# A two-part layer on one core: early rows from six routing groups, and their timetable one token tile to the front

## The chip, the core and the metric

The kernel runs on one core of a Trainium2 chip. A core has a matmul engine (TensorE, PE; its weight loads are listed as PEld), a vector engine (VectorE, DVE), an activation engine (ScalarE, ACT), GpSimd (POOL) and SyncE (SP), which here issues DMAs; 16 DMA engines move data between HBM and the on-chip memory SBUF. PE writes its results to eight PSUM banks. The metric is the device time of one execution in microseconds (us), lower is better.

## What is computed

Attention (a Nystroem form with landmarks, an iterated inverse and a convolution over the rows), then a mixture of eight experts, each with a residual. In the reference, cut to what matters:

```python
x = x + attention(layernorm(x))                   # x is 4 x 1024 x 256
h = layernorm(x)                                  # 4096 tokens of 256
logits = h @ router_w.T                           # 8 experts
routing_weights, selected = sparsemixer_eval(logits, 0.01)   # two experts for each token
for e in range(8):
    g = silu(h @ w_gate[e].T) * (h @ w_up[e].T)   # 512 wide
    out = out + dense_w[:, e:e + 1] * (g @ w_down[e].T)
x = x + out
```

All is in float32. Since each token goes to two of eight experts, 8192 rows are sorted by expert and computed in blocks.

## The kernel before

**Token loop.** The last third of the attention and the routing run together in `token_step(i)`, written out for each engine. Each batch of 1024 rows has 9 query tiles (CT = 9, QT = 36 in all). In step i PE computes the scores of query tile i (`c2_sim`, L1730), the convolution with the values of tile i - 2 (`c2_conv`, L1775), and the output product y of a row tile of 128 rows (`c2_y`, L1783, `y_step(m)` is the step of row tile m). Every ninth step (12, 21, 30) has no y tile. DVE takes the maxima and sums of the softmax (L1210, L1213, L1220, L1226), and adds y to the residual: that is x1(m), `rows_out`, L1111, with the statistics behind it. ACT takes the exponentials and moves the convolution out of PSUM, GpSimd weighs (`weigh`, L571) and adds the bias to the residual rows (`add_bias`, L577), which x1(m) waits for.

**Routing.** Row tiles form nine groups (`GROUPS`): 0 to 6 have four tiles, 7 and 8 have two. `DONE[g]`, called D in this document, is the step of the last y tile of group g: 7, 11, 16, 20, 25, 29, 34, 36, 38. `LATE` is 6. Behind it come, for groups 0 to 5: the deviations (`inverse_deviations`, DVE, L1124 to L1132) and the normalised rows (`norm_rows`, ACT, L774) in step D+1; on PE two pairs of transposes (`c2_tp`, L1743), h = 0 in D+2 and h = 1 in D+3, each with its logits (`c2_lg`, L1751); the choice of the experts (`choices`, DVE, L1165 to L1177, with the logits transposed back on PE, L1765) in step `CHOSEN` = D+4; the counts (`c2_counts`, PE, L1801) in `COUNTED` = D+5; the slots of the rows (`take_counts` and `slots`, DVE, L1153 and L1184 to L1203) in `PLACED` = D+6; and from there the scatter of the rows to their expert's region of xs_d in HBM (`scatter`, GpSimd, L585), two tiles in step `PLACED` and two in the next. `sent_at` moves those that fall in steps 35 to 37 one step on. Group 6 has its transposes in D+1 and D+2, and its choice, counts and slots in steps 36, 37 and 37.

**Early rows.** The expert with most rows after the first `EARLY + 1` groups (`choose_early`, DVE, L1233 to L1240, behind the slots of group `EARLY`) surely has `EROWS` rows by then: a whole number of 128-row tiles. Two steps behind `PLACED[EARLY]` SP loads this expert's weights and these rows (`first_rows`, L413 to L420), once the groups' scatters have landed. They are computed around the end of the token loop, while the last groups are still being placed.

**Experts.** The rest of the rows is computed in items, in an order fixed ahead (`KIND`), whose expert and address are read from tables: units (two 128-row tiles of one expert, two steps), tiles (128 rows, part-full, one step) and quads (four pieces of 32 rows, one step). `ITEMS` has the steps of each item, `NU` and `NT` the numbers of units and tiles that suffice for any routing. A step has gate and up products (`hidden`, L1887) and a down product (`down`, L1930), an item the transposes of its rows (`x_columns`, L1850). For a unit the gate and up products have 256 moving columns, for a tile 128 and twice as many instructions. DVE weighs the products (L1301), and GpSimd adds them to the output in HBM (`add_rows`, L606); an item's adds wait until those of the item ahead have landed.

With EARLY = 4, EROWS is 640: two units and one single tile (5 steps). Then come 22 units, 6 quads and 11 tiles, the last five items being tiles: 5 + 44 + 6 + 11 = 66 steps.

The order on each engine is the order of the code. What runs ahead is set by semaphores alone.

## Time and profile before

| | |
|---|---|
| median of three runs | 1118.95 us (1118.33 to 1119.6) |
| profiled execution | 1113.18 us, its span 1111.4 us |
| PE busy | 96% of the span |
| PEld, DVE, ACT, POOL busy | 77%, 58%, 29%, 27% |
| DMA | 68.27 MB, mean 61 GB/s |
| PE's chain: gate and up (L1887), down (L1930) | 221.9 us and 113.9 us |
| PE: scores L1730, y L1783, convolution L1775 | 129.7, 120.2 and 65.1 us |

The span runs from the first to the last instruction; times in the rows are us from its start. The token loop lies from about 410 to 724, the expert stage behind it. A row of a timeline merges neighbouring instructions of one kind. In brackets stands the idle time of the engine ahead of it and whose work ended it. PEclk is the granted share of TensorE's full clock.

### The profile page before, as it was taken

How to read it: one execution, taken by the hardware profiler on the slowest of the kernel's cores; microseconds unless marked ns; L12 is line 12 of the kernel's file. 1: busy time of each engine (PE TensorE's matmuls, PEld its weight loads, DVE VectorE, ACT ScalarE, POOL GpSimd, SP SyncE). 2: the span in 40 equal slices, each digit the busy share in tenths (PEclk: the TensorE clock that was granted, in tenths of full speed). 3: DMA queues.
4: the chain of work that ended last, by engine and by line, in shares of the span. 5: the costliest groups of instructions: out<-in, count | busy, mean ns of one | idle time of the engine just before them, and what ended most of it. 6: DMA issues, size and time to landing. Idle time of an engine off the chain costs nothing. (4 is left out here: it accounts for less than half of the span.)

```text
span 1111.4 us, 22942 instructions
## 1 busy us (share of the span) xinstructions
PE 1069.8 (96%) x9126; PEld 859.7 (77%) x9126; DVE 641.6 (58%) x1376; ACT 319.2 (29%) x471; POOL 301.2 (27%) x303
## 2 busy tenths in 40 slices
PE   4999999999999999999999999999999999999996
PEld 4888888888888756667766666788887877878895
DVE  7457756655558576677677777875334434343332
ACT  4433232222224423332332342331122122121210
POOL 6000000000020013225435435462332333333333
PEclk9999999999999999999999999999999999999999
DMA  9300000000300040321322224235423233333122
GB/s 336 127 1 1 1 1 1 1 1 1 97 3 0 2 191 20 106 67 64 126 80 68 97 66 129 87 134 103 86 48 49 46 45 52 49 51 46 20 30 24
DMA packets 48253, 68.27 MB, mean 61 GB/s; under 512 B 8225, under 2 KB 41505, under 8 KB 47137
## 3 DMA queue, kind: packets, MB, share of 16 engines
q1 hardware_dynamic: 34288, 46.83, 13.4%
q0 software_dynamic: 13440, 16.93, 9.2%
q10 hardware_dynamic: 432, 3.24, 0.7%
q8 instruction: 62, 1.02, 0.4%
q14 instruction: 31, 0.25, 0.1%
HBM read 41.43 MB, written 26.59 MB: 61 GB/s over the span
## 5 line engine op out<-in xcount | busy, mean ns | idle before, releaser
L1887 PE MATMUL ps<-mem 128*128 128x256 f32 (+1 forms) x1152 | 221.9, 345 | 0.0
L1887 PEld LDWEIGHTS ps<-mem 128*128 128x128 f32 x1152 | 190.1, 191 | 27.2 <-issue 7.5
L606 POOL DMA_INDIRECT out<-mem x60 | 102.6, 1710 | 188.8 <-DVE mem L1301 139.7
L571 POOL TENSOR_TENSOR mem<-mem,small 128x1024 f32<-128x1024 f32 x36 | 68.6, 1905 | 241.9 <-DVE small L1223 112.0
L1289 DVE TENSOR_TENSOR mem<-mem,ps 128x512 f32<-128x512 f32 x66 | 45.4, 687 | 150.5 <-PE ps L1887 129.8
L1730 PE MATMUL ps<-mem 128*128 128x512 f32 x288 | 129.7, 594 | 0.0
L1783 PE MATMUL ps<-mem 128*128 128x256 f32 x512 | 120.2, 388 | 0.0
L818 ACT ACTIVATE mem<-ps 128x512 f32<-128x512 f32 x66 | 39.4, 597 | 278.5 <-PE ps L1887 250.4
L1480 PE MATMUL ps<-mem 128*128 128x256 f32 x512 | 117.3, 382 | 0.6 <-ACT mem L692 0.6
L1930 PE MATMUL ps<-mem 128*128 x480 | 113.9, 380 | 1.8 <-DVE mem L1289 1.8
L1441 PE MATMUL ps<-mem 128*128 128x256 f32 x512 | 114.5, 380 | 0.0
L1783 PEld LDWEIGHTS ps<-mem 128*128 128x128 f32 x512 | 95.8, 192 | 16.3 <-issue 4.3
L1441 PEld LDWEIGHTS ps<-mem 128*128 128x128 f32 x512 | 95.6, 190 | 12.7 <-issue 0.3
L1480 PEld LDWEIGHTS ps<-mem 128*128 128x128 f32 x512 | 94.8, 190 | 13.5 <-issue 0.8
L1930 PEld LDWEIGHTS ps<-mem 128*128 128x128 f32 x480 | 88.3, 190 | 12.9 <-issue 2.5
L1730 PEld LDWEIGHTS ps<-mem 128*128 128x128 f32 x288 | 54.2, 190 | 54.8 <-issue 52.7
L585 POOL DMA_INDIRECT xs_d<-mem,idx x64 | 62.3, 974 | 40.2 <-DVE idx L1203 23.9
L1775 PEld LDWEIGHTS ps<-mem 128*64 128x64 f32 x1152 | 57.1, 137 | 18.3 <-issue 18.3
L1775 PE MATMUL ps<-mem 128*64 128x116 f32 x1152 | 65.1, 266 | 0.8 <-POOL mem L571 0.8
L1318 DVE COPY mem<-mem 128x2048 f32 x51 | 62.0, 1235 | 5.9 <-issue 3.1
L793 ACT ACTIVATE mem<-ps 128x928 f32<-128x928 f32 (+2 forms) x36 | 31.5, 874 | 103.0 <-PE ps L1775 103.0
L1301 DVE TENSOR_SCALAR mem<-ps,mem 128x256 f32<-128x256 f32 x66 | 29.7, 480 | 46.7 <-PE ps L1930 46.4
(237 smaller groups left out, 1388.0 us busy)
## 6 DMA issues: line engine op xcount, KB each, us to landing
mem<-w_gu SPq DMA_DIRECT2D x9, 1024.0 KB, 5.6
mem<-xs_d SPq DMA_DIRECT2D x22, 260.0 KB, 2.8
mem<-x SPq DMA_DIRECT2D x8, 512.0 KB, 8.2
mem<-x SPq DMA_DIRECT2D x32, 128.0 KB, 2.3
out<-mem SPq DMA_DIRECT2D x32, 128.0 KB, 1.7
mem<-w_down SPq DMA_DIRECT2D x8, 512.0 KB, 5.5
xnt_d<-mem ACTq DMA_DIRECT2D x3, 1056.0 KB, 5.3
mem<-xnt_d SPq DMA_DIRECT2D x3, 1056.0 KB, 4.9
```

The costliest lines, as they stand in the source:

```text
L571: pool.tensor_tensor(a1[:, u], ex[:, u].rearrange("p (h c) -> p h c", h=H), ri[:, 16 * u:16 * u + 16].unsqueeze(2).to_broadcast([P, H, M]) ...
L585: pool.indirect_dma_start(out=xs_d, out_offset=bass.IndirectOffsetOnAxis(ap=idx[:, u, v, c:c + 1].bitcast(U32), axis=0), in_=xd[:, u, v, c ...
L606: pool.indirect_dma_start(out=out_rows, out_offset=bass.IndirectOffsetOnAxis(ap=rows_to.bitcast(U32), axis=0), in_=ys[:, r % YRING], in_of ...
L1289: dve.tensor_tensor(hid[:, n % 2], sil[:, n % 2], bank(2 + n % 2), ALU.mult).then_inc(s("m_hid"), 1)
L1318: dve.tensor_copy(v, w_gu_s[:, e]).then_inc(s("m_w"), 1)
L1441: mm = pe.matmul(bank(t // 2)[:, t % 2 * 2 * P:(t % 2 + 1) * 2 * P], xnts[b][:, k, HALO + P * t:HALO + P * t + P], g3c[:, b, k, j * P:(j + ...
L1480: mm = pe.matmul(bank(6)[:, k * 2 * P:(k + 1) * 2 * P], xna[:, b, t, k * P:(k + 1) * P], e3s[m % 4][:, t], start=(t == 0), stop=(t == RT - 1))
L1730: mm = pe.matmul(bank(2 * u + half), xnt2[b % 2][:, k, TO * t:TO * t + P], g1c[:, b, k, 512 * half:512 * half + 512], start=(k == 0), stop ...
L1775: mm = pe.matmul(bank(4, 2)[c:c + 64, (h // 2) * P:(h // 2) * P + TO], a1[:, q % 2, h], band[:, h], start=True, stop=True)
L1783: mm = pe.matmul(bank(6)[:, 0:D], cvt[:, j, at_:at_ + P], pm[:, b, j], start=(j == 0), stop=(j == J - 1))
L1887: mm = pe.matmul(bank(2 * c + n % 2)[:, i * size:(i + 1) * size], w[:, k, c, f * P:(f + 1) * P], xst[:, a % 2, k, 0:size], start=(k == 0), ...
L1930: mm = pe.matmul(bank(down_bank(a, b))[:, 0:D], hid[:, u, i * size + b * P:i * size + (b + 1) * P], w_d_s[:, e, f], start=(f == 0), stop=( ...
```

## The change

`EARLY` becomes 5: six groups are placed before the early rows are taken, so `EROWS` is 768, six tiles in three units. The rows left shrink by 128, so `NT` goes from 11 to 10 (the last four items are tiles); NU and the quads stay. The steps are 6 + 44 + 6 + 10 = 66. `choose_early` moves to group 5's slots, the early loads to two steps behind them. `CHOSEN`, `COUNTED` and `PLACED` of groups 0 to 5 are each one step less, and their transposes and logits stand where those of group 6 stood: h = 0 in D+1, h = 1 in D+2.

```diff
-EARLY = 4
+EARLY = 5
...
-CHOSEN = [i + 4 for i in DONE[:LATE]] + [QT, QT + 2, QT + 4]
-COUNTED = [i + 5 for i in DONE[:LATE]] + [QT + 1, QT + 3, QT + 5]
-PLACED = [i + 6 for i in DONE[:LATE]] + [QT + 1, QT + 4, QT + 5]
+CHOSEN = [i + 3 for i in DONE[:LATE]] + [QT, QT + 2, QT + 4]
+COUNTED = [i + 4 for i in DONE[:LATE]] + [QT + 1, QT + 3, QT + 5]
+PLACED = [i + 5 for i in DONE[:LATE]] + [QT + 1, QT + 4, QT + 5]
...
-                return i + 1 if QT - 1 <= i <= QT + 1 else i
+                return i + 1 if QT <= i <= QT + 1 else i
...
@@ token_step of the tensor engine (ACT's norm_columns move alike)
-                for h in range(2):
-                    for g in groups_at(DONE[:LATE], i - 2 - h):
-                        c2_tp(g, h)
                 for g in groups_at(CHOSEN[:LATE], i):
                     c2_logit_rows(g)
-                if i == DONE[LATE] + 2:
-                    c2_tp(LATE, 1)
-                    pe.wait_ge(s("c2_sub"), QT - 1)
-                    c2_lg(LATE, 0)
+                for g in groups_at(DONE[:LATE + 1], i - 2):
+                    c2_tp(g, 1)
+                    if g < LATE:
+                        bank6_read(i)
+                    else:
+                        pe.wait_ge(s("c2_sub"), QT - 1)
+                    c2_lg(g, 0)
                 if 0 <= i - 2 < QT:
                     c2_conv(i - 2)
-                if i == DONE[LATE] + 1:
-                    c2_tp(LATE, 0)
-                if i == DONE[LATE] + 2:
-                    c2_lg(LATE, 1)
+                for g in groups_at(DONE[:LATE + 1], i - 1):
+                    c2_tp(g, 0)
+                for g in groups_at(DONE[:LATE + 1], i - 2):
+                    c2_lg(g, 1)
                 bank6_read(i)
-                for h in range(2):
-                    for g in groups_at(DONE[:LATE], i - 2 - h):
-                        c2_lg(g, h)
...
             hidden(0, 4)
             down(3)
+            hidden(1, 4)
+            hidden(0, 5)
             x_columns(3)
-            hidden(1, 4)
+            down(4)
+            hidden(1, 5)
```

ACT gets `gate_out(5)` and DVE `hidden_out(5)` for the sixth early step. The kernel after has other line numbers: DVE's 2 lower (L1111 is L1109), PE's 1 lower in the token loop.

Three places in the order of the engines. First DVE in step 35, before, from the subtraction of the maxima of step 34 to the slots of group 5:

```order
L1213 TENSOR_TENSOR mem<-ps,small 128x1024 [waits c2_a1,dve_chain]
L1111 TENSOR_TENSOR mem<-ps,mem 128x256 [waits x1_out3,c2_norm,c2_xrb,c2_y]
L1116 BN_STATS small<-mem 128x6 [waits c2_x1]
...
L1132 SCALAR_TENSOR_TENSOR small<-small 128x4 [waits dve_chain]
L1153 COPY mem<-ps 128x64 [waits d_cnt]
L1220 TENSOR_REDUCE small<-mem 128x16 [waits c2_exp]
L1226 RECIPROCAL small<-small 128x16 [waits dve_chain]
L1210 TENSOR_REDUCE small<-ps 128x16 [waits c2_sim]
L1213 TENSOR_TENSOR mem<-ps,small 128x1024 [waits c2_a1,dve_chain]
L1184 TENSOR_TENSOR mem<-mem 128x64 [waits d_exp]
```

And the same place after, from the subtraction of step 34 to x1(27) of step 35:

```order
L1211 TENSOR_TENSOR mem<-ps,small 128x1024 [waits c2_a1,dve_chain]
L1182 TENSOR_TENSOR mem<-mem 128x64 [waits d_exp]
...
L1201 CAST idx<-mem 128x2x4 [waits dve_chain]
L1231 TENSOR_TENSOR small<-run,small 128x8
...
L1238 SCALAR_TENSOR_TENSOR small<-small 128x8 [waits dve_chain]
L1109 TENSOR_TENSOR mem<-ps,mem 128x256 [waits x1_out3,c2_norm,c2_xrb,c2_y]
L1114 BN_STATS small<-mem 128x6 [waits c2_x1]
```

The slots of group 5 (17 instructions) and the choice of the early expert (8) stand ahead of x1(27) now; the slots stood behind the subtraction of step 35, the choice in step 31.

Second GpSimd in steps 34 to 38 (L571 weighs, L577 adds a bias, L585 scatters a tile to one of its two experts), as the difference:

```order
 L571 TENSOR_TENSOR mem<-mem,small 128x1024
 L577 TENSOR_TENSOR mem<-mem 128x256
+L585 DMA xs_d<-mem,idx 33920x260 x4
 L571 TENSOR_TENSOR mem<-mem,small 128x1024
 L577 TENSOR_TENSOR mem<-mem 128x256
 L585 DMA xs_d<-mem,idx 33920x260 x4
-L577 TENSOR_TENSOR mem<-mem 128x256
-L585 DMA xs_d<-mem,idx 33920x260 x4
-L577 TENSOR_TENSOR mem<-mem 128x256
+L571 TENSOR_TENSOR mem<-mem,small 128x1024
+L577 TENSOR_TENSOR mem<-mem 128x256 x3
 L585 DMA xs_d<-mem,idx 33920x260 x16
```

Group 5's scatters stand in steps 34 and 35, where they stood in 36 and 37; those of groups 6 to 8 stay.

Third SP, where the early weights (w_gu) and early rows (xs_d) are loaded, in the kernel after (L409 stores a row tile, L400 loads down weights):

```order
L400 DMA mem<-w_down 128x1024 x2
L409 DMA out<-mem 128x256
L414 TENSOR_LOAD early
L414 ISA x2
L415 ISA
L415 DMA mem<-w_gu 128x2x1024
L419 TENSOR_LOAD early
L419 ISA x2
L420 ISA
L420 DMA mem<-xs_d 128x6x260
L409 DMA out<-mem 128x256 x3
```

The two early loads stood ahead of the stores of row tiles 26 and 27, in step 33, with 5 tiles of rows; they stand now in step 36, behind the store of row tile 28.

## Rows read from the trace of the kernel before

**Rows 1.** The page: busy us of each engine, share of the span, instructions.

```profile
PE 1069.8 (96%) x9126; PEld 859.7 (77%) x9126; DVE 641.6 (58%) x1376; ACT 319.2 (29%) x471; POOL 301.2 (27%) x303
```

**Rows 2.** Timeline, PE, expert stage: start us, us, engine, line, operation, operands, count.

```profile
1042.31 3.62 PE L1887 MATMUL ps<-mem 128*128 128x256 f32 x16
...
1053.11 3.62 PE L1887 MATMUL ps<-mem 128*128 128x256 f32 x16
...
1074.77 3.73 PE L1887 MATMUL ps<-mem 128*128 128x128 f32 x32
...
1080.29 3.73 PE L1887 MATMUL ps<-mem 128*128 128x128 f32 x32
```

**Rows 3.** Timeline, PE, end of the token loop; in brackets idle time and releaser.

```profile
672.27 0.60 PE L1743 MATMUL ps<-ids,mem 128*128 128x128 f32 x4
...
702.15 0.66 PE L1743 MATMUL ps<-ids,mem 128*128 128x128 f32 x4
...
715.99 0.41 PE L1801 MATMUL ps<-mem,tri 128*128 128x32 f32 x2 [0.48 <-DVE mem L1111]
...
721.48 0.66 PE L1743 MATMUL ps<-ids,mem 128*128 128x128 f32 x4 [1.33 <-ACT mem L774]
722.92 1.03 PE L1759 MATMUL ps<-rw,mem 128*128 128x8 f32 x8 [0.78 <-ACT mem L782]
723.80 0.93 PE L1850 MATMUL ps<-ids,mem 128*128 128x128 f32 x4
```

**Rows 4.** Windows of core 0: length, busy us of PE, PEld, DVE, ACT, POOL, PEclk, DMA, GB/s.

```profile
112.00:114.00 2.00, 0.49 (x3) 0.20 (x2) 1.59 (x3) 0.97 (x2) 0.00 (x0) 1.00 0.00 0
720.00:724.00 4.00, 1.89 (x15) 1.53 (x15) 3.56 (x20) 2.03 (x3) 3.06 (x5) 1.00 0.28 100
724.00:728.00 4.00, 4.00 (x14) 3.36 (x13) 2.64 (x16) 1.39 (x3) 3.22 (x4) 0.57 0.39 134
```

**Rows 5.** Timeline, DVE, token steps 30 to 37.

```profile
660.55 0.21 DVE L1153 COPY mem<-ps 128x64 f32<-128x64 f32 x1
...
668.86 0.16 DVE L1233 TENSOR_TENSOR small<-run,small 128x8 f32<-128x8 f32 x1
...
670.31 0.42 DVE L1111 TENSOR_TENSOR mem<-ps,mem 128x256 f32<-128x256 f32 x1
...
697.06 0.42 DVE L1111 TENSOR_TENSOR mem<-ps,mem 128x256 f32<-128x256 f32 x1 [3.35 <-PE ps L1783]
...
704.34 0.50 DVE L1184 TENSOR_TENSOR mem<-mem 128x64 f32<-128x64 f32 x1
...
707.58 0.42 DVE L1111 TENSOR_TENSOR mem<-ps,mem 128x256 f32<-128x256 f32 x1
...
710.62 1.90 DVE L1165 SCALAR_TENSOR_TENSOR mem<-mem 128x32 f32<-128x32 f32 x1
...
715.51 0.42 DVE L1111 TENSOR_TENSOR mem<-ps,mem 128x256 f32<-128x256 f32 x1
```

**Rows 6.** Timeline, ACT, token step 35: normalising of group 6.

```profile
700.57 2.93 ACT L774 ACTIVATE mem<-mem,small 128x512 f32<-128x512 f32 x4 [5.71 <-DVE small L1132]
```

**Rows 7.** Timeline, GpSimd (POOL), weighing in token steps 32 and 36.

```profile
674.60 1.91 POOL L571 TENSOR_TENSOR mem<-mem,small 128x1024 f32<-128x1024 f32 x1
...
710.58 1.90 POOL L571 TENSOR_TENSOR mem<-mem,small 128x1024 f32<-128x1024 f32 x1 [5.83 <-DVE small L1223]
```

**Rows 8.** Timeline, SP's queue: early weights and early rows.

```profile
681.55 0.40 SPq L415 DMA_DIRECT2D mem<-w_gu  x1
688.00 0.39 SPq L420 DMA_DIRECT2D mem<-xs_d  x1
```

**Rows 9.** DMA issues by line: size of one, median us to landing.

```profile
mem<-xs_d SPq DMA_DIRECT2D x1, 650.0 KB, 4.5
```

**Rows 10.** Timeline of all engines, last product on DVE and last add on GpSimd.

```profile
1101.54 0.48 DVE L1301 TENSOR_SCALAR mem<-ps,mem 128x256 f32<-128x256 f32 x1 [2.18 <-PE ps L1930]
1103.80 1.55 POOL L606 DMA_INDIRECT out<-mem  x1 [3.14 <-DMA out<-mem]
```

More of the change, by code:

```diff
@@ L836, in _ @@
             for i in range(QT + 2):
-                for h in range(2):
-                    for g in groups_at(DONE[:LATE], i - 2 - h):
-                        norm_columns(g, h)
-                if i == DONE[LATE] + 2:
-                    norm_columns(LATE, 1)
+                for g in groups_at(DONE[:LATE + 1], i - 2):
+                    norm_columns(g, 1)
                 if QT <= i < QT + 2:
@@ L850, in _ @@
                     conv_out(i - 2)
-                if i == DONE[LATE] + 1:
-                    norm_columns(LATE, 0)
+                for g in groups_at(DONE[:LATE + 1], i - 1):
+                    norm_columns(g, 0)
                 if i < QT:
@@ L868, in _ @@
             gate_out(4)
+            gate_out(5)
             rows_transposed(3)
@@ L1365, in _ @@
             hidden_out(4)
+            hidden_out(5)
             for n in range(BLOCK[FIRST], NSTEP):
@@ L1809, in token_step @@
                     c2_sim(i)
-                for h in range(2):
-                    for g in groups_at(DONE[:LATE], i - 2 - h):
-                        c2_tp(g, h)
                 for g in groups_at(CHOSEN[:LATE], i):
                     c2_logit_rows(g)
-                if i == DONE[LATE] + 2:
-                    c2_tp(LATE, 1)
-                    pe.wait_ge(s("c2_sub"), QT - 1)
-                    c2_lg(LATE, 0)
+                for g in groups_at(DONE[:LATE + 1], i - 2):
[5 more added lines that the diff above has]
+                    c2_lg(g, 0)
                 if 0 <= i - 2 < QT:
                     c2_conv(i - 2)
-                if i == DONE[LATE] + 1:
-                    c2_tp(LATE, 0)
-                if i == DONE[LATE] + 2:
-                    c2_lg(LATE, 1)
+                for g in groups_at(DONE[:LATE + 1], i - 1):
+                    c2_tp(g, 0)
+                for g in groups_at(DONE[:LATE + 1], i - 2):
+                    c2_lg(g, 1)
                 bank6_read(i)
-                for h in range(2):
-                    for g in groups_at(DONE[:LATE], i - 2 - h):
-                        c2_lg(g, h)
                 for g in groups_at(COUNTED, i):
```

## The prediction

> **What bounds the kernel now.** Read the page first: PE is busy for 1069.8 us of the span [rows 1], at the full granted clock nearly everywhere, so the time is PE's work plus the places where PE waits. PE's starts in the expert stage give the price of a step [rows 2]. Its timeline at the end of the token loop shows where it waits [rows 3], the windows what the clock does behind those waits [rows 4], and the other engines' timelines who was late [rows 5 to 7]. I name token steps by i, and x1(m) is the DVE addition that finishes row tile m, y(m) PE's product for it.
>
> **Early rows: three units, ten part-full tiles.** The number of 128-row steps stays 66: before 5 early + 44 unit + 6 quad + 11 tile, after 6 + 44 + 6 + 10. Two steps with 128 moving columns (one early, one late) become one unit of two steps with 256 columns. Single steps start 5.52 us apart (1080.29 - 1074.77), a unit takes 10.80 us (1053.11 - 1042.31), 5.40 for each of its steps [rows 2]. All of it is PE time on the path: 2 x (5.52 - 5.40) = **0.24 us gained**. DVE saves one weight copy, which lies beside PE's work and is worth nothing. Bounds: 0 and 0.3.
>
> **The timetable, steps 7 to 33.** PE gets the same transposes, logits and counts, in other steps. Groups 0 to 5 now have their first transpose in step D+1, D being the step of their last y tile, as group 6 had before. There it fits to 0.1 us: ACT starts normalising at 700.57, half of its 2.93 us is needed, that is 702.04, and PE starts the transpose at 702.15 with no idle time [rows 3, 6]. Six such places, 0 to 0.1 us each with DVE on time: I take **0.2 us lost** in all.
>
> Groups 0, 2 and 4 are placed in the step without a y tile (12, 21, 30), together with the deviations of the next group. GpSimd waits there for the slots, issues four scatters, and only then weighs and adds the bias of the next y tile. For step 30: before, DVE could have begun the slots when it took the counts at 660.55 [rows 5]. Now the counts are taken ahead (0.2) and PE's earlier counts shift all by 0.5, so they run from 661.2 to 664.3 at most. The next weighing on GpSimd came 5.74 us behind the end of the slots (674.60 - 668.86) [rows 5, 7], so 670.0 now; it and the bias take 1.9 + 0.7, then x1(24) and the copy of the logits 0.7: 673.3. PE comes to the transposed logits at 672.27 [rows 3] plus the 1.1 us of group 5's second transposes (0.60) and logits (I take 0.5) that now stand ahead: 673.4. **No wait, by 0.1 us**; bounds 0 and 3 x 0.5.
>
> **The end of the loop, steps 34 to 37.** Before, group 5's slots stand in DVE's step 35, behind the deviations of group 6, for 3.24 us (704.34 to 707.58) [rows 5]. They move to step 34, and the choice of the early expert follows them there: 1.45 us (668.86 to 670.31) [rows 5]. In step 34 DVE had been idle for 3.35 us ahead of x1(27) at 697.06 [rows 5], so since 693.7. PE's counts of group 5 now come a step earlier, which shifts this to 694.1; slots, 3.0 to 3.2, and the choice then end at 698.4. x1(27) starts at 698.4 instead of 697.06, **1.35 us late**, and nothing hides that: the deviations, the normalising and the transpose of group 6 stand directly behind it, 5.1 us from x1 to transpose (697.06 to 702.15), with 0.1 us of slack. PE waits **1.3 us** in step 35 where it did not wait. Bounds 0.8 and 2.0.
>
> Behind that DVE is rid of the slots. Before: x1(28) at 707.58, x1(29) at 715.51, when PE had already finished y(29) and the convolution behind it; PE waited 0.48 us for it at 715.99 and 1.33 us at 721.48 for the normalising of group 7 [rows 3, 5]. After: PE is 1.3 us later, DVE not, so x1(29) starts between 715.2 and 716.3, and 5.1 us behind it, between 720.3 and 721.4, the transpose of group 7 could start. PE itself gets there at 721.48 - 1.81 + 1.3 = 721.0. So the transpose starts between 721.0 and 721.4 where it was 721.48: the 1.81 us of waits shrink to 0 to 0.4, but the new 1.3 us stand before them. **0.3 us gained** net, bounds 0.8 gained and 0.7 lost.
>
> In x1(29)'s delay one DVE instruction of 1.90 us stands (710.62), while GpSimd's weighing ran from 710.58 to 712.48 [rows 5, 7]. The Trainium skill (GPSIMD Engine Reference, Key points) says that GpSimd shares its SBUF interfaces with VectorE, in contention with Vector instructions that take two SBUF inputs; this trace agrees. By that rule the three bias additions that now stand behind each other on GpSimd would slow DVE there a little more; that stays inside the bound of 716.3.
>
> **The clock.** Between 720 and 724 PE is busy for only 1.89 us, and from 724 to 728 the granted clock is 0.57 on average, with the lower of the two levels (1.2 GHz) for most of it [rows 4]: 4 x 0.43 = **1.7 us lost**. After, the idle time there is 0 to 0.4 ahead of the transpose and 0.78 behind it [rows 3], about 1 us instead of 2.1. A stretch of 2 us with 1.51 idle, 112 to 114, had a full clock behind it [rows 4]. So I expect the fall to be gone: 1.7 us gained. Other bound: 0, it stays.
>
> **The early rows' load.** It was issued at 688.00, 6.45 us behind the early weights (681.55), and landed 4.5 us later, 30 us ahead of its use at 723.80 [rows 3, 8, 9]. After, both are asked for behind the store of x1(28), which ends near 708.0; the weights followed the store by some 2 us, so 709.9, and the rows 716.3. With 768 rows instead of 640 they take 4.5 to 5.4 us: landed between 720.8 and 721.8. PE wants them at 723.5. **Hidden, with 1.7 us left** of 30.
>
> **The tail.** The last DVE product started at 1101.54 and took 0.48; GpSimd's last add to memory started at 1103.80 [rows 10], 1.78 us behind: its chain of adds was still catching up with PE from the last unit. With four tiles behind that unit instead of five it has one period less. **0.4 us lost**, bounds 0 and 0.7.
>
> **Sum** against the profiled execution (1113.18 us, span 1111.4): -0.24 + 0.2 - 0.3 - 1.7 + 0.4 = -1.6. The median of the three runs, 1118.95, stands 5.8 above the profiled one; the same step from it gives **1117.3 us**.
>
> **Rivals.**
> (1) The clock still falls. One row with a similar idle share and no fall behind it is thin evidence. All else as above: +0.1, **1119.0 us**. The Trainium skill (TensorE: Matmul & The Clock Gate, HAM oscillation) tells of engines that fall to the lower level over and over from waits between short bursts of matmuls; the row of 720 agrees, that of 112 shows that not each gap does it.
> (2) Slower: the early rows come late. Stores, scatters and 1 MB of weights share the DMA engines, and it decides from 1.7 us of delay on. Each microsecond beyond stalls PE at 723.5 with nothing beside it, and the clock falls as before. At 4 us late: +0.1 + 2.3, **1121.4 us**.
> (3) Slower, on DVE: it is later than I work out, 0.5 us at each of the three transposed logits and 2.0 at group 6, the clock fall kept: +0.1 + 1.5 + 0.7, **1121.3 us**.
> (4) Faster: the wait at group 6 is only 0.5 and both old waits go: -1.6 - 0.9, **1116.5 us** or less.
> (5) The change does not do what it says. The order shows the six tiles and the moved rows, so that is no case of its own.
>
> **How the numbers follow.** The forecast has 0.45, (1) 0.22, (2) 0.08, (3) 0.10, (4) 0.15. A measurement of this kernel can tell about 0.2%, 2.2 us, from no change: faster is below 1116.7, slower above 1121.2. Faster: most of (4) and the lower part of the forecast's own spread of 1 us to each side, 0.24. Slower: most of (2), half of (3), 0.13. Within: 0.63. The range, 1115.0 to 1121.3, takes in the bounds of the terms and leaves out the ends of (2), (3) and (4).
>
> **What would show it.** Right: PE idle for 1 to 1.5 us by ACT's normalising ahead of group 6's first transpose; none at the counts of group 6; no window with a clock of 0.50 behind 720; four single steps last, 5.52 us apart; early rows landed between 720 and 722. Wrong: PE waiting at the early rows' transposes, or at the transposed logits of steps 14, 23 and 32; a clock fall in another place, such as behind the new wait at 702.

## The result, and the profile after

| | median of 20 executions | profiled execution, its span |
|---|---|---|
| before | 1118.72 us (1117.21 to 1119.85) | 1113.18, 1111.4 us |
| after | 1122.78 us (1118.73 to 1124.72) | 1123.47, 1121.7 us |

The ratio is 1.003, 95% interval 1.0023 to 1.0037: the kernel after is 0.3% slower. Five of its 20 executions lie between 1118.7 and 1119.2, fifteen between 1121.9 and 1124.7. I call these two kinds the lower and the upper cluster. The forecast was 1117.3, with a range that ended at 1121.3; by the prediction's own borders 1122.8 is slower, for which it had a chance of 0.13.

First PE's timeline of after, all places from 718 to 760 where it waited (start us, us, engine, line, operation, operands, count, in brackets the idle time and its releaser), ahead of them the one in step 35. In such brackets `remote` is a releaser that the profile can't name, `issue` a gap in which the engine waited for nothing that the profile shows.

```profile
703.75 0.66 PE L1742 MATMUL ps<-ids,mem 128*128 128x128 f32 x4 [1.50 <-ACT mem L774]
...
718.37 0.41 PE L1800 MATMUL ps<-mem,tri 128*128 128x32 f32 x2 [0.62 <-DVE mem L1109]
722.96 0.66 PE L1742 MATMUL ps<-ids,mem 128*128 128x128 f32 x4 [0.42 <-ACT mem L774]
724.40 1.03 PE L1758 MATMUL ps<-rw,mem 128*128 128x8 f32 x8 [0.78 <-ACT mem L782]
734.48 0.66 PE L1742 MATMUL ps<-ids,mem 128*128 128x128 f32 x4 [1.30 <-ACT mem L774]
738.84 1.06 PE L1758 MATMUL ps<-rw,mem 128*128 128x8 f32 x8 [1.97 <-DVE mem L1151]
755.55 3.78 PE L1926 MATMUL ps<-mem 128*128 x8 [3.88 <-DVE mem L1287]
```

With 0.89 us at 792.15 together 11.4 us. The trace of before has 0.48, 1.33, 0.78 [rows 3], and behind them 1.36 and 0.90, 4.9 us in all. So 6.5 of the 10.3 us between the two profiled executions are waits, and 5.85 us of the waits stand at two places that no step of the prediction has, 738.84 and 755.55. The second, ahead of a down product (L1926), I call the wait at down.

The windows of after (length, busy us of PE, PEld, DVE, ACT and POOL, PEclk, DMA share, GB/s) show the clock. It doesn't fall between 720 and 728, where it fell before [rows 4], but behind the wait at 755:

```profile
720.00:724.00 4.00, 3.19 (x16) 2.32 (x14) 3.47 (x23) 1.86 (x3) 0.00 (x0) 1.00 0.27 95
724.00:728.00 4.00, 3.60 (x23) 3.38 (x24) 3.45 (x18) 0.85 (x2) 2.08 (x3) 1.00 0.19 66
...
756.00:760.00 4.00, 4.00 (x11) 3.10 (x11) 1.09 (x1) 0.54 (x2) 0.00 (x0) 0.50 1.02 282
760.00:764.00 4.00, 4.00 (x16) 3.38 (x15) 1.27 (x2) 0.00 (x0) 0.00 (x0) 0.78 0.42 145
```

That is 4.00 x 0.50 + 4.00 x 0.22 = 2.9 us of PE's busy time lost, where before lost 1.7. The rest is the tail, 1.6 us (below), and small terms.

**Where the 3.88 us come from.** The timeline of all engines of after at that place. PE's row of 24 matmuls is three products of 8, 1.73 us apart (745.90 to 751.08): the gate product of early step 2, its up product, the gate product of step 3.

```profile
745.90 5.34 PE L1883 MATMUL ps<-mem 128*128 128x256 f32 x24
746.64 0.96 POOL L585 DMA_INDIRECT xs_d<-mem,idx  x1 [1.09 <-issue]
...
751.70 1.63 POOL L606 DMA_INDIRECT out<-mem  x1 [0.30 <-issue]
751.73 0.60 ACT L818 ACTIVATE mem<-ps 128x512 f32<-128x512 f32 x1 [5.91 <-PE ps L1883]
753.64 1.58 POOL L606 DMA_INDIRECT out<-mem  x1 [0.30 <-issue]
754.71 0.69 DVE L1287 TENSOR_TENSOR mem<-mem,ps 128x512 f32<-128x512 f32 x1 [2.87 <-remote]
```

And the same place before, where ACT starts 1.92 us behind the start of the gate product and DVE 4.72 behind it:

```profile
743.93 5.34 PE L1887 MATMUL ps<-mem 128*128 128x256 f32 x24
744.60 0.96 POOL L585 DMA_INDIRECT xs_d<-mem,idx  x1 [2.83 <-DVE idx L1203]
745.85 0.60 ACT L818 ACTIVATE mem<-ps 128x512 f32<-128x512 f32 x1 [2.00 <-PE ps L1887]
...
748.65 0.68 DVE L1289 TENSOR_TENSOR mem<-mem,ps 128x512 f32<-128x512 f32 x1
```

After, ACT should start at 745.90 + 1.92 = 747.8 and starts at 751.73, 3.9 us late, though it had been idle for 5.91 us; DVE takes the up product, ended by 749.5, at 754.71. PE can't go on without DVE's result. Nothing on ACT or DVE stands in the way. What does go on is GpSimd: six indirect DMAs in a row, 746.64 to 755.22, group 8's scatters and the first two early adds. Both starts, 751.73 and 754.71, lie inside this row, not behind it.

The cleanest case is in the middle of the token loop of after, where it costs PE nothing:

```profile
672.58 1.01 POOL L585 DMA_INDIRECT xs_d<-mem,idx  x1 [0.17 <-issue]
673.53 1.81 PE L1774 MATMUL ps<-mem 128*64 128x116 f32 x32
676.43 0.96 POOL L585 DMA_INDIRECT xs_d<-mem,idx  x1 [0.30 <-issue]
678.37 0.95 ACT L793 ACTIVATE mem<-ps 128x928 f32<-128x928 f32 x1 [9.36 <-remote]
```

PE's convolution ends at 675.34, ACT takes it at 678.37, 3.0 us later and 1.0 us behind the end of GpSimd's row of four (677.39). I call this a **late release**: an engine is idle, the result that it waits for has ended, and it starts over 1 us later.

### The profile page after: what moved, and what is told of

Its sections match the earlier page's. It is cut to its first block and busy times, and to the rows that moved or that the text cites. A ratio compares the mean times of both kernels' runs of the same rounds, so it can differ in the third digit from the quotient of the medians.

```text
span 1121.7 us, 22865 instructions
## 1 busy us (share of the span) xinstructions
PE 1070.3 (95%) x9094; PEld 857.5 (76%) x9094; DVE 642.4 (57%) x1375; ACT 318.7 (28%) x470; POOL 301.1 (27%) x303
## 5 line engine op out<-in xcount | busy, mean ns | idle before, releaser
L571 POOL TENSOR_TENSOR mem<-mem,small 128x1024 f32<-128x1024 f32 x36 | 68.6, 1906 | 226.3 <-DVE small L1221 120.7
L1926 PE MATMUL ps<-mem 128*128 x480 | 115.6, 384 | 5.7 <-DVE mem L1287 5.7
L1926 PEld LDWEIGHTS ps<-mem 128*128 128x128 f32 x480 | 89.5, 192 | 17.3 <-issue 6.3
L585 POOL DMA_INDIRECT xs_d<-mem,idx x64 | 62.4, 975 | 57.7 <-DVE idx L1201 40.7
```

The costliest lines, as they stand in the source:

```text
L571: pool.tensor_tensor(a1[:, u], ex[:, u].rearrange("p (h c) -> p h c", h=H), ri[:, 16 * u:16 * u + 16].unsqueeze(2).to_broadcast([P, H, M]) ...
L585: pool.indirect_dma_start(out=xs_d, out_offset=bass.IndirectOffsetOnAxis(ap=idx[:, u, v, c:c + 1].bitcast(U32), axis=0), in_=xd[:, u, v, c ...
L1926: mm = pe.matmul(bank(down_bank(a, b))[:, 0:D], hid[:, u, i * size + b * P:i * size + (b + 1) * P], w_d_s[:, e, f], start=(f == 0), stop=( ...
```

## The experiments

Two theories. **H**: some results of PE that end while GpSimd issues indirect DMAs back to back reach the other engines only about 1 us behind the end of the row. **A**: the DMA traffic of those stretches (1 MB weights at 710 and at 730, rows, stores) holds them. And for the part of the change at fault: the timetable, or six groups with their later loads. The number of executions stands in the text where it is small (4 to 6). In the tables below, "before" is the kernel before on the same chip, in the same set.

### Set 1: repeats, the timetable alone, the weights sooner

| before 1118.21 us | median | ratio (95%) |
|---|---|---|
| before_again | 1118.03 | 1.0004 (0.9994 to 1.0013) |
| after_again | 1120.67 | 1.0014 (1.0003 to 1.0025) |
| time_only | 1115.26 | 0.9982 (0.9969 to 0.9995) |
| weights_ahead | 1120.40 | 1.0018 (1.0002 to 1.0033) |

**before_again**, no edit.

> The kernel before once more, unchanged, for a second profiled execution. The one shown (1113.18 us) lies 5.5 us under the median of its runs (1118.7). If that is a plain offset of profiling, this one is near 1113 again and PE's waits behind 700 are those of before (0.5 to 1.4 us each, clock at 0.50 for 3.4 us). If before too has executions in which PE waits for late releases, as the profiled execution of after does (1.97 us at 738.8 and 3.88 us at 755.6), then it is near 1118 and shows at least 3 us of such waits that the first lacked, in the same place.

PE's timeline, its longest waits:

```profile
721.69 0.65 PE L1743 MATMUL ps<-ids,mem 128*128 128x128 f32 x4 [2.09 <-ACT mem L774]
725.27 1.85 PE L1759 MATMUL ps<-rw,mem 128*128 128x8 f32 x8 [2.93 <-ACT mem L782]
738.88 0.66 PE L1743 MATMUL ps<-ids,mem 128*128 128x128 f32 x4 [2.23 <-ACT mem L774]
```

With 0.48 us at 715.43 and 0.65 at 754.28 these are 8.4 us where the trace shown of before has 4.0 at the same places, and as PE was 0.6 us ahead at 715, the two spans differ by 4.4 us. The granted clock is 0.50 from 724 to 728, with PE busy for 2.73 us, and 0.67 to 732, with PE busy throughout: 1.4 + 1.3 = 2.7 us lost instead of 1.7. The timeline of its other engines tells why:

```profile
713.14 1.81 PE L1775 MATMUL ps<-mem 128*64 128x116 f32 x32
...
716.60 0.96 POOL L585 DMA_INDIRECT xs_d<-mem,idx  x1 [0.30 <-issue]
...
719.28 0.81 ACT L793 ACTIVATE mem<-ps 128x768 f32<-128x768 f32 x1 [9.62 <-remote]
...
722.30 0.96 POOL L585 DMA_INDIRECT xs_d<-mem,idx  x1 [0.30 <-issue]
...
724.53 0.60 ACT L782 ACTIVATE mem<-ps 128x512 f32<-128x512 f32 x1 [2.90 <-remote]
```

The convolution ended at 714.95 and is taken at 719.28, 1.7 us behind the end of four scatters of group 5 (712.76 to 717.56). The transposes of 721.69 ended at 722.34 and ACT takes them at 724.53, 1.3 us behind the end of the other four (718.49 to 723.26); PE's 2.93 us at 725.27 are a wait for this copy. (x1(30), 5.0 us behind the end of y(30), is no such case: DVE has no idle time ahead of it, it works on group 6's slots until 724.57.) So the usual execution of before has late releases, at 1118 us, and the profiled one from which I predicted has none, at 1113. The second branch of the expectation came true.

**after_again**, no edit.

> The kernel after once more, unchanged. Its 20 runs lie in two clusters, 1118.7 to 1119.2 (5 runs) and 1121.9 to 1124.7 (15 runs). If the waits at 738.8 and 755.6 with the clock fall behind them (1.97 + 3.88 + 3.4 us) are what divides them, a profile of the lower cluster lacks the second wait and its fall, one of the upper cluster has both. Median 1122.8 again, 1.003 of before.

Its profiled execution (1122.59 us) again has the wait at down (3.86 us). The median expected, 1122.8, did not come: of its 11 executions six lie over 1120.6 and five under 1119.2, so the shares of the two clusters vary from set to set, and the median with them. A profile of the lower cluster came in set 5.

**time_only**, the timetable with EARLY = 4:

```diff
-EARLY = 5
+EARLY = 4
```

with PE's, ACT's and DVE's early steps as before.

> The timetable of after alone: groups 0 to 5 one step to the front, but EARLY = 4, so 640 early rows, eleven tiles, early weights and rows loaded by SP in step 32. Theory A (the crowded DMA engines: weights, rows and stores that after has between 710 and 735 delay PE's results there): the loads are at their old place, the late waits at 738 and 755 are gone, 1117.5 to 1119. Theory B (the timetable itself: DVE and ACT reach the end of the loop in another order): the waits and the clock fall stay, 1122 to 1124.

1115.26, faster than before, and 5.4 us faster than after in the same set. The timetable is a gain; the loss is in the other part. PE's waits:

```profile
720.76 0.66 PE L1740 MATMUL ps<-ids,mem 128*128 128x128 f32 x4 [0.43 <-ACT mem L774]
722.20 1.03 PE L1756 MATMUL ps<-rw,mem 128*128 128x8 f32 x8 [0.78 <-ACT mem L782]
...
736.64 1.06 PE L1756 MATMUL ps<-rw,mem 128*128 128x8 f32 x8 [1.86 <-DVE mem L1150]
```

The 2.09 and 2.93 us of before_again are 0.43 and 0.78. The 1.86 us at 736.64 come from a late release (the up product that DVE takes at 734.77, shown in set 2), and theory A missed here: it said that they would go. B missed by the time. Nor is there a wait in step 35.

**weights_ahead**, after with the early weights asked for a step sooner:

```diff
+                if i == PLACED[EARLY] + 1:
+                    first_weights()
                 if i == PLACED[EARLY] + 2:
                     first_rows()
```

> After, with one edit: SP asks for the early weights (1 MB) one step sooner, in step 35 instead of 36, so that they land near 706 and not 716; the early rows stay in step 36. Theory A: with 1 MB less behind 710 the late releases shrink, the median falls by 2 us or more, to 1119 to 1121. Theory B: no change, 1122 to 1124.

The weights were issued at 703.4 instead of 710.7. 1120.40 alone would fit A's range, but after itself took 1120.67 in this set: 1.0018 beside 1.0014, no gain. In its trace the up product of early step 0 is still late by 4.1 us. The first blow to A.

### Set 2: the choice, the adds, and a broken row

| before 1118.55 us | median | ratio (95%) |
|---|---|---|
| choice_later | 1119.71 | 1.0011 (1.0002 to 1.0020) |
| adds_later | 1117.85 | 0.9995 (0.9987 to 1.0004) |
| time_adds | 1115.56 | 0.9976 (0.9967 to 0.9986) |
| series_split | 1113.31 | 0.9960 (0.9946 to 0.9974) |

**choice_later**, on after:

```diff
+                if i == PLACED[EARLY] + 1:
+                    choose_early()
                 for g in groups_at(PLACED, i):
                     slots(g)
-                    if g == EARLY:
-                        choose_early()
```

> After, with the choice of the early expert (8 DVE instructions, 1.45 us) moved from step 34 to the end of DVE's step 35, behind the deviations of group 6. My step of the prediction: these 1.45 us and the slots make x1(27) late, and PE waits 1.5 us in front of group 6's first transpose (703.75). If so, that wait falls to 0.3 us or less, and the median of after falls by 1 to 1.5 us, to about 1119.5 to 1121. If the wait is set by something else (a release held back), it stays at 1.5.

(After itself was not run in set 2; the kernels of this set stand beside before.) PE's first transpose of group 6 now starts without a wait (the row has no bracket):

```profile
701.10 0.66 PE L1742 MATMUL ps<-ids,mem 128*128 128x128 f32 x4
```

The named cause of that wait is right. The median is where it was expected, and executions up to 1121.9 remain, so this is not the main loss.

**adds_later**, on after:

```diff
             for r in range(EBLK):
-                wait_alone(pool, "m_y", r + 1)
+                wait_alone(pool, "m_y", max(r, 2) + 1)
```

> After, with one edit on GpSimd: the adds of the first two early blocks wait until the third block is weighed, so that they don't follow group 8's scatters without a gap. In after GpSimd issues 6 indirect DMAs in a row from 746.6 to 755.2, PE's first gate product of step 2 ends at 747.8 and ACT gets it at 751.7, the up product ends at 749.5 and DVE gets it at 754.7. Theory H (PE's results reach the others only about 1 us behind the end of such a row of issues): the row now ends near 751.4, DVE starts by 753.2, PE's wait of 3.9 us falls to 2.4 or less, median 1119.5 to 1121.5. Theory A (DMA traffic of any kind): little changes, since the four scatters and the loads stay, 1120.7 to 1123.

1117.85, the slowest of 11 at 1119.02: the upper cluster is gone, more than H had asked for. The timeline:

```profile
746.95 5.34 PE L1883 MATMUL ps<-mem 128*128 128x256 f32 x24
747.55 0.96 POOL L585 DMA_INDIRECT xs_d<-mem,idx  x1 [2.62 <-DVE idx L1201]
748.88 0.60 ACT L818 ACTIVATE mem<-ps 128x512 f32<-128x512 f32 x1 [2.00 <-PE ps L1883]
```

Here the gate product that ends 1.3 us into the row is released at once, though in after one that ended 1.1 us into it was held. So not every result in a row is held. The late adds are not what this trace shows: traces of after without them have the same place without a wait (set 5), where as here the row starts 2.6 us or more behind the one ahead of it, 1.1 in after. The times carry the reading: 11 of 11 executions are of the lower cluster, beside 5 of 20, 5 of 11, 1 of 5 and 7 of 12 of after in other sets. Through what the late adds do it is open: they shorten the row by 3.9 us, and other timings may have moved as well.

**time_adds**, the same edit on time_only.

> The timetable alone (EARLY = 4) with the same edit on GpSimd's first adds. Theory H: the executions of the slower cluster (1117.4 to 1120.2, 4 of 12) lose their excess, the others stay at 1114 to 1115.6: median 1114.5 to 1115.3. Theory A: the same as the timetable alone, 1115.3.

1115.56 beside 1115.26: no gain for the median. The slowest of 9 is 1117.44 where time_only had 1120.2; the expected lower median did not come, and the two highest values alone, in 9 and 12 executions, don't show that a slower cluster went. No trace was taken of a slow execution of time_only.

**series_split**, on time_only: ahead of the seventh of group 6's eight scatters GpSimd waits for PE's up product of early step 0.

```diff
                             scatter(g, 2 * h)
+                            if g == LATE and h == 1:
+                                wait_alone(pool, "m_up", 1)
                             scatter(g, 2 * h + 1)
```

> The timetable alone (EARLY = 4), with group 6's eight scatters split: behind the fourth GpSimd waits for PE's up product of early step 0 (m_up), which ends at 730.6 and reached DVE only at 734.8, 1.7 us behind the end of the row of eight (723.1 to 733.0). Theory H: with the row ended at 728.1 the product reaches DVE at once, at 730.7, four microseconds sooner. Theory A (the 1 MB weight load issued at 728.0 holds it): it still comes near 734, and GpSimd's last four scatters with it. The median is open, 1113 to 1117: the last four scatters come later.

(The text says that the wait stands behind the fourth scatter; as written it stands behind the sixth.) This is the experiment that decides between H and A, by one trace of each kernel. First time_only, where the row is whole, then series_split; in both the products of early step 0 (16 matmuls: gate, then up) and the weight load on SP:

```profile
727.01 3.62 PE L1881 MATMUL ps<-mem 128*128 128x256 f32 x16
728.04 0.44 SPq L397 DMA_DIRECT2D mem<-w_gu  x1
732.01 0.96 POOL L585 DMA_INDIRECT xs_d<-mem,idx  x1 [0.30 <-issue]
734.77 0.69 DVE L1286 TENSOR_TENSOR mem<-mem,ps 128x512 f32<-128x512 f32 x1 [4.09 <-remote]
```

```profile
728.79 3.62 PE L1883 MATMUL ps<-mem 128*128 128x256 f32 x16
729.60 0.96 POOL L585 DMA_INDIRECT xs_d<-mem,idx  x1 [0.31 <-issue]
729.82 0.45 SPq L397 DMA_DIRECT2D mem<-w_gu  x1
...
732.64 0.69 DVE L1288 TENSOR_TENSOR mem<-mem,ps 128x512 f32<-128x512 f32 x1
733.42 0.96 POOL L585 DMA_INDIRECT xs_d<-mem,idx  x1 [2.85 <-PE ps L1883]
```

With the whole row the up product ends at 730.63 and DVE takes it at 734.77, 1.8 us behind the row's end (732.97). With the row ended at 730.56 it ends at 732.41 and DVE takes it at 732.64. The 1 MB load runs in both (a load of this size took 5.6 us in the trace of before). So A falls, and H stands in this: without the row the product is not held. In two traces of set 4 with the same edit the product ends only 0.2 us behind the shortened row, and DVE takes it 1.3 us later, 1.5 behind the row's end.

H does not stand to the letter, since releases come inside a row too. In time_only ACT takes the gate product of this step, ended at 728.90, at 730.34, 2.6 us ahead of the row's end; and in after the two starts of the wait at down, 751.73 and 754.71, lie in the row.

The median is 1113.3, from 4 executions. Beside time_adds, in the same set, that is 0.9960 to 0.9976, and the two intervals overlap: the trace shows the release, the times alone do not settle what it is worth.

### Set 3: no late releases

| before 1112.61 us | median | ratio (95%) |
|---|---|---|
| time_split_adds | 1111.68 | 0.9993 (0.9981 to 1.0005) |
| six_groups_clear | 1112.52 | 0.9997 (0.9988 to 1.0007) |
| before_split_adds | 1112.69 | 0.9999 (0.9988 to 1.0009) |

time_split_adds is time_only with both edits on GpSimd (the broken row, the later adds); six_groups_clear is after with these two and choice_later's; before_split_adds is before with the two.

> The timetable alone (EARLY = 4) with both edits on GpSimd: group 6's row of eight scatters is broken (it waits for PE's first up product ahead of the last two), and the first adds wait for the third early block. Theory H (a result of PE that ends inside a long row of GpSimd's indirect DMAs reaches the others only behind the row): 1112.6 to 1114, no slower cluster; PE's waits behind 735 are 1 us in all.

> After (EARLY = 5) with the three edits that each take one cause away: the choice of the early expert in step 35, group 6's row broken, the first adds later. What is left between this and the timetable alone with the same edits is what six groups and 768 rows cost or bring by themselves. If only the tail does (last add 5.4 us behind PE's last product in after, 3.7 in before) less the 0.24 us of the tiles, it is 1 to 2 us slower than that kernel: 1114.2 to 1115.5. If it is equal to it, the early rows were slow through the three causes alone; if it is over 3 us slower, a cause is still missing.

> Before, with the same two edits on GpSimd. In a usual execution of before PE waits 2.09 us (721.7), 2.93 us (725.3) and 2.23 us (738.9). The first two lie in the row of scatters of group 5 that the timetable moves away, and stay; the third and a part of the clock fall go: 1115.5 to 1117.5. Should it come to 1113, the timetable has no gain of its own over the broken rows.

Here the kernel before itself took 1112.6, the time of the profiled execution of before, and the edits brought nothing (1111.7 to 1112.7). That all three ratios are 1 fits H if there is nothing here to take away, and the three profiled executions show no late release. No wait in them has the releaser `remote`, nor has one in the trace shown of before, where the other 16 traces have 4 to 10 each. Set 3 ran on the same chip as set 2, so it is not the chip alone. What makes the difference, the runs don't tell. The kernels of this set are in sets 4 and 5 again, and so the same program can be compared with and without late releases. In six_groups_clear ACT takes the convolution of step 32 0.05 us behind its end (674.87):

```profile
674.92 0.94 ACT L795 ACTIVATE mem<-ps 128x928 f32<-128x928 f32 x1 [6.38 <-PE ps L1776]
```

In six_groups_clear_2, the same program with the same row of four scatters beside it, it ends at 675.35 and is taken at 678.36. A row of indirect DMAs alone is thus not enough for a late release.

### Set 4: the same with late releases

| before 1117.81 us | median | ratio (95%) |
|---|---|---|
| after_third | 1121.90 | 1.0035 (1.0022 to 1.0047) |
| time_only_2 | 1117.55 | 0.9993 (0.9981 to 1.0006) |
| time_split_adds_2 | 1113.41 | 0.9964 (0.9951 to 0.9977) |
| six_groups_clear_2 | 1113.21 | 0.9967 (0.9956 to 0.9979) |

> The kernel after, unchanged, beside the three below. Where before takes 1112 to 1113 us (PE's results reach the others at once, as in the trace shown of before), the steps of my prediction should hold but for the tail: 1112 to 1113.5, within 0.1% of before, with no wait over 1.6 us and one cluster. Where before takes 1118, it is 1120 to 1123 with two clusters, as twice before.

> The timetable alone, once more. Where before takes 1112 to 1113: 1111 to 1112.5, ratio 0.999 to 1.000. Where before takes 1118: 1115.3, ratio 0.997 to 0.998.

> The timetable alone with both edits on GpSimd, once more, since the first time before stood at 1112.6, where there is nothing for the edits to take away (0.9993). Where before takes 1118: 1112.6 to 1114, ratio 0.995 to 0.9965. Where it takes 1112 to 1113: the same as the timetable alone.

> After with the three edits, once more. Where before takes 1118: 1113.5 to 1115.5, so 0.5 to 2 us slower than the timetable alone with the two edits, and 5 us or more faster than after. Where it takes 1112 to 1113: 0.8 us slower than the timetable alone with the two edits, as the first time.

Here after_third and time_split_adds_2 have 5 executions each, six_groups_clear_2 has 6. after_third again has the wait at down, 4.54 us. The three edits take 8.7 us from it, and what is left is within the intervals of the timetable alone with its two edits: of the expected 0.5 to 2 us for six groups and 768 rows nothing shows in the medians, though these intervals, 1.2 us to each side, don't exclude a part of it. PE's longest waits in six_groups_clear_2 are 1.30 us (732.53) and 1.51 us (749.00). Late releases remain in it and in time_split_adds_2: DVE takes the counts of group 8 1.9 and 1.8 us behind their end.

time_only_2 missed: 1117.55, not 1115.3, with 7 of 12 executions at 1117 to 1119.6 that were 4 of 12 the first time. Its gain over before lies between 0 and 3 us, by the share of such executions, and what makes them slow no trace shows.

### Set 5: the rest

| before 1118.45 us | median | ratio (95%) |
|---|---|---|
| after_fourth | 1118.83 | 1.0015 (0.9999 to 1.0032) |
| six_split_adds | 1115.74 | 0.9978 (0.9965 to 0.9990) |
| before_split_adds_2 | 1117.55 | 0.9990 (0.9980 to 1.0000) |

> The kernel after, unchanged. Where before takes 1117 to 1119: 1121 to 1123. Where before takes 1112 to 1113, which after has not yet been run beside: 1112 to 1114 if the held releases carry its loss (the wait by ACT's normalising of 1.5 us and a tail 1 to 1.5 us longer stay, the clock fall at 724 goes), 1117 or more if they don't.

> After with the two edits on GpSimd, but the choice of the early expert left in step 34. Beside six_groups_clear_2 (1113.2, 0.9967 of before) it prices the 1.5 us wait in front of group 6's first transpose: 1114.5 to 1115, 0.998 of before, where before takes 1118.

> Before with the two edits on GpSimd, once more, since the first time before itself took 1112.6 and there was nothing to take away (0.9999). Where before takes 1118: its waits of 2.1 and 2.9 us at 721 and 725 lie in the row of group 5's scatters, which the edits don't break, so 1115.5 to 1117.5; at 1113.4 the timetable would have no gain of its own over them.

after_fourth missed its median (1118.83, not 1121 to 1123): it has seven executions from 1116.5 to 1118.9 and five from 1121.9 to 1124.3. The profiled one is of the lower cluster (1118.81), and what it lacks is the wait at down. First a window with its granted clock (columns as in the windows of after), then the place itself:

```profile
740.00:744.00 4.00, 4.00 (x17) 3.47 (x18) 3.38 (x22) 0.44 (x2) 1.83 (x2) 0.69 0.09 33
```

```profile
749.81 0.96 POOL L585 DMA_INDIRECT xs_d<-mem,idx  x1 [3.19 <-DVE idx L1201]
750.58 0.60 ACT L818 ACTIVATE mem<-ps 128x512 f32<-128x512 f32 x1 [2.00 <-PE ps L1883]
...
754.69 1.99 PE L1926 MATMUL ps<-mem 128*128 x8 [0.26 <-DVE mem L1287]
```

0.26 us instead of 3.88. The lower cluster has a clock fall too, but another one: 0.69 here and 0.88 in the next 4 us, 1.7 us lost, where after has 1.00 until the wait at down and loses 2.9 behind it. The wait (3.6 less) and the clock (1.2 less) come to 4.8 us, beside 4.7 between the two profiled executions.

The fall comes first in time and may be what decides. With it PE is later beside GpSimd, the counts of group 8 come when group 7's row is over, and group 8's row starts 3.19 us behind it; in after 1.09. All seven traces of kernels with six groups and group 6's row whole fall in line: four have a clock fall behind 736 or 740, a gap of 2.6 to 3.2 us and no wait at down (after_fourth, weights_ahead, choice_later, adds_later), three have no fall there, a gap of 1.1 us and a wait of 3.9 to 4.5 us (after, after_again, after_third). This order is read from the traces; no run sets the clock or the gap by itself.

six_split_adds is after with the two edits on GpSimd and the choice left in step 34: 0.9978 beside the 0.9967 of six_groups_clear_2, so the choice costs some 0.0011 of 1118, 1.2 us. The two come from different sets and their intervals overlap, so this size is an estimate; that the wait is there with the choice in step 34 and gone with it in step 35, 1.50 against 0.23 us or less, the traces show. Its median, 1115.74, is above the 1114.5 to 1115 expected.

before_split_adds_2 came just past the upper end of its expectation. Its two long waits are not in group 6's row: they are 2.13 us (721.71) and 2.92 us (725.28), as in before_again, and only the third fell, from 2.23 to 1.30 us (738.99). Even that brought PE nothing there: its transposes started at 738.88 in before_again, since the clock took back what the wait gave (0.50 from 728 to 732, where it was 0.67). The two long waits are gone in the kernels with the timetable, which moves group 5's scatters ahead of them. Breaking group 5's row in before, which would test this alone, was not run.

## Why the prediction was wrong, step by step

**What bounds the kernel.** Right in kind, but read from an execution that is not the usual one. It lay 5.8 us under the median of the runs shown. I took that for an offset and put my -1.6 onto the median. It was the sign of 4.4 us more of waits and 1.0 more of slow clock (before_again), and of a mechanism of which the trace shown has no instance. That is the step that failed, "the same step from it gives 1117.3": every term of the sum is a difference in a program without late releases. In its place the runs showed a wait of 3.9 to 4.5 us at down, which the sum does not have, with 1.2 us more lost to the clock, in a part of the executions.

**Tiles, -0.24.** Nothing contradicts it; it is too small to be seen alone.

**The timetable, steps 7 to 33, +0.2.** Scores of step 35 start at 696.91 after and 0.05 us sooner before, while the start of the loop is 0.21 sooner after: 0.3 lost. No wait at the transposed logits. Right.

**End of the loop.** x1(27) was to start at 698.4 and started at 698.43; the wait was to be 1.3 us and is 1.50 in the profile, and the medians put it at some 1.2 (set 5). The two old waits were to shrink to 0 to 0.4 and are 0.62 and 0.42. With the 1.50 that is 2.54 where 1.81 stood, so 0.7 lost instead of 0.3 gained, the end of its bounds. Against the usual before, whose waits there are 0.48, 2.09 and 2.93, the timetable gains several microseconds that the sum did not have.

**The clock, -1.7.** The fall behind 724 is gone in the profiled execution of after, and there in those of after_again and after_third, 1.6 us lost in each (0.85 and 0.72 from 724 to 732 in the first). So this term's other bound came true in two of four traces. In after it came back behind 755, twice as long: 1.2 us more lost than before, where 1.7 were to be gained.

**The early rows' load.** Issued at 716.70 (forecast 716.3), 5.0 us, wanted at 725.28: hidden with 3.6 us left where 1.7 were forecast. Right, and weights_ahead shows that its earlier half is worth nothing.

**The tail, +0.4.** Mis-sized too: the last add starts 3.86 us behind the last product on DVE, 2.26 before [rows 10], so +1.6. The timeline of DVE and GpSimd:

```profile
1110.19 0.48 DVE L1299 TENSOR_SCALAR mem<-ps,mem 128x256 f32<-128x256 f32 x1 [2.18 <-PE ps L1926]
1114.05 1.55 POOL L606 DMA_INDIRECT out<-mem  x1 [3.13 <-DMA out<-mem]
```

Each add waits for the landing of the one ahead, 4.6 to 4.7 us apart, beside PE's steps of 5.5 [rows 2]: 0.8 us are caught up a step, and there is one step less; that is already twice what I took. One landing more was slow (4.86 us of waiting ahead of the add at 1104.78, where 3.1 is usual). It is no chance of one trace: the ten traces with six groups have 3.2 to 3.9 us from the last product on DVE to the last add, the ten with five groups 1.3 to 2.3. In set 4 these 1.0 us did not show in the median; six_groups_clear_2 has its last product 0.5 us sooner than time_split_adds_2.

**Rivals.** None was the cause. Rival (3), DVE later than worked out, had the right sign, but DVE was not late by its own work: x1(27) came when forecast, and at the wait at down DVE was released late. Rival (1), the clock still falls, happened in after_again and after_third, but it was to give 1119.0 and they took 1122.6 and 1123.2. Rival (2) did not happen. There was no case for a mechanism that the trace of before does not show; with all three runs shown 5 us over the profiled one, it should have had a chance of its own and widened the range.

**In sum**, the loss of after against the timetable alone (5.4 us in set 1, 4.4 in set 4) has two named parts: the wait at down with its clock fall, in 5 of 12 to 4 of 5 executions (adds_later, 0.9995 beside 1.0014 to 1.0035), and the choice of the early expert in step 34 (some 1.2 us). With these and the row of group 6 out of the way, the change with its edits is a gain, 0.9967 of before where late releases are, and time_split_adds_2 (0.9964) and series_split (0.9960), with five groups, can't be told from it.

**Open.** Why a chip or a set of executions has late releases and another has none; which results in a row are held, and when in it they are let go; what makes some executions of time_only slow; and what the kernel after takes where there are no late releases, since it was not run there. That the forecast would have held there is so not shown.

## To carry to other kernels

When the profiled execution is faster than all timed ones by several times their spread, take a second trace before pricing anything: the difference is itself a mechanism, and the change may act on it. Look in a trace for instructions that wait long and start well behind the end of the product they wait for, with a releaser that is unknown, and see what GpSimd does meanwhile. A long row of indirect DMAs beside a stretch where PE waits for what others make of its results is worth an attempt to break it with one wait: with the two other edits it took 8.7 us from after in set 4, in before it brought 0.9 us with the later adds (0.9990, with an interval up to 1.0000), and without late releases nothing.

## What the runs showed of the hardware

- **Late releases.** PE's finished results reached ACT and DVE up to 4.3 us late: convolutions 3.0 and 4.3 us, an up product 4.1, a pair of transposes 2.2, these 1.0 to 1.8 us behind the end of a row of four to eight indirect DMAs of GpSimd, each 0.96 us and 1.27 apart. Others came inside a row, the gate product of the wait at down 3.9 us late. With the row ended ahead of it the product was released in 0.2 us. The Trainium skill (SBUF — State Buffer, Who interferes with whom) tells of contention between GpSimd and VectorE on their shared interfaces, and that DMA never contends with a compute engine. This is about the ports of SBUF and names no case in which GpSimd's DMAs delay what waits for PE; the runs show one. By what path it happens they don't tell.
- **It is there or not as a whole.** Before takes 1118 us in four sets and 1112.6 in one, the two on one chip among them (sets 2 and 3), and the trace shown belongs with the second. The same program with the same row of scatters has its convolution taken 0.05 us behind its end in set 3 and 3.0 us behind it in set 4.
- **The clock.** Two kernels with the same busy share in the same stretch: series_split, then time_only (windows as above).

```profile
720.00:724.00 4.00, 2.79 (x19) 2.18 (x19) 3.54 (x21) 1.41 (x3) 0.78 (x1) 0.94 0.07 26
724.00:728.00 4.00, 4.00 (x13) 3.24 (x13) 2.03 (x12) 2.11 (x3) 3.09 (x4) 0.64 0.31 109
```

```profile
720.00:724.00 4.00, 2.79 (x21) 2.20 (x20) 3.54 (x21) 1.55 (x4) 0.88 (x1) 1.00 0.09 32
724.00:728.00 4.00, 4.00 (x20) 3.54 (x19) 2.69 (x14) 1.86 (x3) 3.00 (x4) 1.00 0.29 103
```

PE is busy for 2.79 of 4 us in both; in the first the clock falls to the lower level (1.2 GHz) behind it, in the second it stays at 2.4. The idle time in such a stretch alone does not decide whether the clock falls, so a forecast by it should keep both cases open.
